# A graph-attention layer on one core: low parts of V summed by one wide product in ten of 32 row tiles

## The chip, the cores and the metric

The kernel runs on one core of a Trainium2 chip. The metric is the device time of one execution in microseconds (us); a time is the median of several runs. A profile is one further execution, recorded by the hardware profiler.

## The reference, cut to what matters

```python
h = jnp.maximum(_layernorm(x, axis=-1), 0.0)          # x is 4096 x 128
h = h @ W.T + b_W
e = (h @ a1)[:, None] + (h @ a2)[None, :] + b_a[0]    # 4096 x 4096
e = jnp.where(e > 0, e, 0.2 * e)
scores = jnp.where(adjacency_matrix > 0, e, -9e15)
attention = jax.nn.softmax(scores, axis=1)
out = x + attention @ h
```

## The kernel before, in words

The 4096 rows of the output are 32 row tiles of 128, in four groups of eight (`GI`, `NG`). For each group the kernel walks over 16 pairs of neighbour tiles (`PAIRS`), so there are 64 pairs in all, numbered `m`. One pair is a piece of the transposed adjacency matrix of 128 x 2048 integers (1 MB), which SP's queue loads. ScalarE (ACT) turns it into a mask (`mask_part`, L379, two halves), VectorE (DVE) makes of mask, a row and a column of exponentials the weights `w` (`weigh`, L459, two halves of 1024), and TensorE (PE) multiplies (`products`, L841 to L847). `w` has four slots (`SLOTS`), so DVE can be up to four pairs ahead of PE; a slot comes free when PE is done with its pair (`mm_done`).

A weight is a 32-bit word that holds two fp16 numbers, a high and a low part, and V (h times the neighbour's factor) is kept in fp16 as a high and a low part too. For each of the 32 neighbour tiles `jt` and each of the eight row tiles `k` of a group PE therefore issues three products with 128 x 128 stationary weights: high weight by high V, high weight by low V, low weight by high V, and all three add up in the same 129 columns of PSUM. The first 128 columns are the sum of rows, the 129th is the sum of the weights, by which the row is divided. V's two parts lie 136 elements apart (`VW`):

```python
nc.tensor.matmul(sums[:, bank, a, :], w16[:, m % SLOTS, col:col + P, 1], V[:, jt, 0, 0:NF], ...)   # L841
nc.tensor.matmul(sums[:, bank, a, :], w16[:, m % SLOTS, col:col + P, 1], V[:, jt, 1, 0:NF], ...)   # L843
nc.tensor.matmul(sums[:, bank, a, :], w16[:, m % SLOTS, col:col + P, 0], V[:, jt, 0, 0:NF], ...)   # L847
```

The order of the work is written out by hand for every engine. In the first 36 us PE also centres x (L805) and makes h (L815), between the first four pairs. DVE prepares exponentials and factors in three parts of the rows (`PARTS`; `scores`, `pack`, `scale_weights`), DVE and ACT make V of the first two chunks (`products` L598, `highs` L369, `lows` L605), GpSimd (POOL) that of the other six (`halves`). In the three later groups DVE inverts the sums of the group before after the first half of pair 5 of a group (`inverse_sums`, L486 to L490); ACT scales its rows out of PSUM after pair 10 (`scale_rows`, L394), POOL adds x (L792), SP stores. The groups alternate between PSUM banks 0 to 2 and 3 to 5; the last has 3 to 7.

The last group ends in pieces: its last three pairs (`ENDS`) are multiplied piece by piece (`PIECES`: 3, 2, 1, 1, 1 row tiles), so that DVE can divide and store one piece (`inverse_last` L504 to L510, `rows` L542) while PE is at the next. Between them DVE tests the sums (`check_sums`, `check_next`, `check_last`), POOL takes the largest of the results, and a flag says whether a slower general form must run, which it doesn't here. The program ends when the stores have landed.

## Time and profile before

| | |
|---|---|
| time, median of 3 runs | 202.33 us (201.9 to 202.39) |
| profiled execution: its own time | 203.52 us |
| profiled execution: span from first to last instruction | 201.9 us |
| PE busy | 197.2 us (98%) |
| DVE busy | 183.1 us (91%) |
| ACT busy | 147.9 us (73%) |
| POOL busy | 53.8 us (27%) |
| moved by DMA | 75.66 MB, mean 375 GB/s |

The profiled execution took 1.62 us more than its span, for what lies around the instructions, and stands 1.19 us above the median of the runs. In the rows, PE is the product itself and PEld the load of its stationary weights; a product is recorded from its start to the modelled end of its result, so that the durations of successive products overlap, and their pace is read from start to start. An fp32 product stands as two records.

### The profile page before, as it was taken

Reading aid. Unit: us, or ns where it says so; the run is one execution under the profiler, and the core shown is the slowest. Engines: PE = TensorE matmul, PEld = TensorE weight load, DVE = VectorE, ACT = ScalarE, POOL = GpSimd, SP = SyncE. Lnnn points to the kernel's source line nnn. Section 1 sums busy time; section 2 is a strip of 40 time slices with the busy share of each in tenths; the row PEclk is TensorE's granted clock in tenths of the full one; section 3 lists DMA queues with packets and bytes.
Section 4 is the critical chain, followed back from the end, with each engine's and each line's share of the span. In section 5 each row is a group of like instructions: output and inputs, shape, how many; then the busy total and the mean of one; then the engine's idle time right before and its main releaser. Section 6 shows DMA issues by size and latency. Waiting matters only on the chain.

```text
span 201.9 us, 7231 instructions
## 1 busy us (share of the span) xinstructions
PE 197.2 (98%) x3183; PEld 190.4 (94%) x3183; DVE 183.1 (91%) x265; ACT 147.9 (73%) x192; POOL 53.8 (27%) x66
## 2 busy tenths in 40 slices
PE   7989999999999999999999999999999999999994
PEld 7558888999999999999999999999999999999994
DVE  4679999999999899987999999989999999999845
ACT  2299988799872777779988688799688888985000
POOL 1000659689997011055000000061000000620000
DMA  5999999999999999999999999999999999996012
GB/s 174 367 412 420 404 411 422 425 406 380 427 428 415 417 424 419 417 425 411 422 419 420 417 417 425 414 420 419 415 419 422 420 414 422 420 356 208 7 38 71
DMA packets 15968, 75.66 MB, mean 375 GB/s; under 512 B 1600, under 2 KB 5952, under 8 KB 7616
## 3 DMA queue, kind: packets, MB, share of 16 engines
q1 hardware_dynamic: 15792, 75.06, 91.3%
q8 instruction: 25, 0.41, 0.8%
q10 hardware_dynamic: 144, 0.13, 0.3%
q14 instruction: 7, 0.06, 0.1%
HBM read 73.08 MB, written 2.11 MB: 372 GB/s over the span
## 4 chain that ended last, share of the span: by engine, by line
PE 97%; ACT 1%; issue 0%; DVE 0%; POOL 0%; POOLq 0%
PE ps L843 29%; PE ps L841 29%; PE ps L847 29%; PE ps L815 4%; PE ps L805 3%; PE ps L857 2%; ACT L411 1%; PE ps L883 1%; ACT hT L335 0%; PE ps L861 0%; PE ps L866 0%; DVE xT L542 0%; PE ps L860 0%; POOL ones L717 0%; ACT warm L411 0%
## 5 line engine op out<-in xcount | busy, mean ns | idle before, releaser
L841 PE MATMUL ps<-V,w 128*128 128x129 f16 x1024 | 174.3, 220 | 0.0
L843 PE MATMUL ps<-V,w 128*128 128x129 f16 x1024 | 174.3, 220 | 0.0
L847 PE MATMUL ps<-V,w 128*128 128x129 f16 x1024 | 174.3, 220 | 0.0
L379 ACT ACTIVATE mask<-adj_sb 128x1024 bf16<-128x1024 int32 x126 | 125.3, 1056 | 27.1 <-DMA adj_sb<-in_adj_t 27.1
L459 DVE SCALAR_TENSOR_TENSOR w<-g_row,pairs,mask 128x1024 f32<-128x1024 f32 x96 | 120.5, 1317 | 5.5 <-ACT mask L379 3.7
L841 PEld LDWEIGHTS ps<-V,w 128*128 128x128 f16 x1024 | 100.2, 98 | 1.5 <-ACT H L340 0.7
L843 PEld LDWEIGHTS ps<-V,w 128*128 128x128 f16 x1024 | 100.2, 98 | 1.0 <-issue 1.0
L847 PEld LDWEIGHTS ps<-V,w 128*128 128x128 f16 x1024 | 100.3, 98 | 0.0
L459 DVE SCALAR_TENSOR_TENSOR w<-ps,pairs,mask 128x1024 f32<-128x1024 f32 x31 | 37.4, 1265 | 0.0
L792 POOL TENSOR_TENSOR xT<-xT,x_sb 128x512 f32<-128x512 f32 x6 | 11.7, 1970 | 76.8 <-ACT xT L394 76.8
L815 PEld LDWEIGHTS ps<-wp,hT 128*128 128x128 f32 x64 | 8.0, 193 | 2.4 <-ACT hT L335 1.7
L805 PE MATMUL ps<-xT,centre 128*128 128x512 f32 x16 | 10.0, 715 | 0.0
L746 POOL TENSOR_TENSOR x_sb<-x_sb,b_row 128x512 f32<-128x512 f32 x8 | 10.0, 1306 | 0.0
L815 PE MATMUL ps<-wp,hT 128*128 128x130 f32 x64 | 8.8, 282 | 0.4 <-ACT hT L335 0.4
L552 DVE BATCH_NORM_STATS2 stats<-x_sb 128x6 f32<-128x128 f32 x32 | 6.8, 280 | 2.5 <-DMA x_sb<-in_x_p 2.5
L761 POOL TENSOR_TENSOR V<-H,evr 128x516 f16<-128x516 f32 (+1 forms) x7 | 6.5, 930 | 5.2 <-DVE evr L591 5.2
L335 ACT ACTIVATE hT<-ps 128x512 f32<-128x512 f32 x8 | 4.7, 588 | 3.7 <-PE ps L805 3.7
L763 POOL TENSOR_TENSOR V<-prod,V 128x516 f16<-128x516 f32 (+1 forms) x7 | 7.0, 1005 | 0.5
L394 ACT ACTIVATE xT<-ps,rg 128x128 f32<-128x128 f32 x24 | 6.5, 381 | 0.0
L762 POOL TENSOR_TENSOR prod<-H,evr 128x516 f32<-128x516 f32 (+1 forms) x7 | 6.5, 925 | 0.0
L795 POOL PARTITION_ALL_REDUCE bad<-bad x1 | 0.4, 380 | 21.7 <-DVE bad L533 21.7
L340 ACT ACTIVATE H<-ps 128x520 f32<-128x520 f32 x8 | 4.7, 593 | 1.6 <-PE ps L815 1.6
(93 smaller groups left out, 62.6 us busy)
## 6 DMA issues: line engine op xcount, KB each, us to landing
adj_sb<-in_adj_t SPq DMA_DIRECT2D x64, 1024.0 KB, 10.5
xT<-in_x_t SPq DMA_DIRECT2D x8, 256.0 KB, 7.2
x_sb<-in_x_p SPq DMA_DIRECT2D x3, 512.0 KB, 10.6
g_row<-g_dram SPq DMA_DIRECT2D x1, 1536.0 KB, 11.0
out<-xT SPq DMA_DIRECT2D x3, 512.0 KB, 9.9
x_sb<-in_x_p SPq DMA_DIRECT2D x2, 256.0 KB, 4.3
out<-xT SPq DMA_DIRECT2D x1, 192.0 KB, 2.0
out<-xT SPq DMA_DIRECT2D x3, 64.0 KB, 1.6
```

The costliest lines, as they stand in the source:

```text
L379: nc.scalar.activation(mask[:, m % MASKS, r], adj_sb[:, m % HELD, r], ACT.Relu, scale=CONNECTED).then_inc(mask_ready, 1)
L394: ins = nc.scalar.activation(Z[:, g, :], sums[:, bank, a, 0:DOUT], ACT.Copy, scale=rg[:, g:g + 1])
L459: nc.vector.scalar_tensor_tensor(w[:, m % SLOTS, side * GC:(side + 1) * GC], g_ps if group == 0 else g_row[:, (group - 1) * GC:group * GC] ...
L552: last = nc.vector.bn_stats(stats[:, g, :], x_sb[:, g, :])
L746: ins = nc.gpsimd.tensor_tensor(x_sb[:, g:g + 4, :], x_sb[:, g:g + 4, :], b_row[:].rearrange("p (a n) -> p a n", a=1).to_broadcast([P, 4, ...
L763: nc.gpsimd.tensor_tensor(V[:, r, 1, 0:NF], prod[:, c % 2, k0:k1, :], V[:, r, 0, 0:NF], ALU.subtract).then_inc(v_ready, 1)
L792: nc.gpsimd.tensor_tensor(Z[:, k, :], Z[:, k, :], x_sb[:, k, :], ALU.add).then_inc(rows_added, 1)
L805: nc.tensor.matmul(ps[:, X_BANK[c], :], centre[:], xT[:, c * CT * P:(c + 1) * CT * P], start=True, stop=True).then_inc(centred, 1)
L815: last = nc.tensor.matmul(ps[:, H_BANK[c] + j // 2, at:at + 2 + DOUT], hT[:, tile * P:(tile + 1) * P], wp[:, WA:WA + 2 + DOUT], start=(j % ...
L841: nc.tensor.matmul(sums[:, bank, a, :], w16[:, m % SLOTS, col:col + P, 1], V[:, jt, 0, 0:NF], start=(jt == 0 and a == 0), stop=False, skip ...
L843: nc.tensor.matmul(sums[:, bank, a, :], w16[:, m % SLOTS, col:col + P, 1], V[:, jt, 1, 0:NF], start=False, stop=False, skip_group_check=True)
L847: last = nc.tensor.matmul(sums[:, bank, a, :], w16[:, m % SLOTS, col:col + P, 0], V[:, jt, 0, 0:NF], start=False, stop=(jt == NT - 1), ski ...
```

## The change

- V's row is laid out anew: 128 low parts, then 128 high parts, then two columns of scale (`NF` is 130 for 128 high parts with the scale), 264 elements in all. The scale is DVE's exponential `ev` itself, as a high and a low fp16 part (`scale_weights`, `ones_low`); before it was a column of H times the same factor as the rest of V. The rest of V is made as before, in 128 columns for 129.
- In ten of the 32 row tiles (`parted`: tile 6 of groups 0 and 2, tiles 0 to 4 of group 1, tiles 0, 2 and 4 of group 3) the products of the high weight with low and high V become one product of 258 columns (`MERGED`), whose low sums stand in 128 PSUM columns of their own. In the other 22 the three products stay, with 130, 128 and 130 columns.
- Groups 1 and 3 now use banks 3 to 7. PE waits for all weights of group 0 before pair 16, since banks 6 and 7 hold a row that `weigh` reads in group 0; and for the scale columns before pairs 0, 4 and 8.
- Of a tile summed apart, ACT scales the low sums too (into `extra`) and POOL adds them; in the last group DVE adds them in `rows`, with a second operation per tile. `inverse_sums` adds the two scale sums with reductions and then inverts; `inverse_last` does so with one operation per tile.
- The pieces of the last group are 2, 2, 2, 1, 1 row tiles.

```diff
-    NF = DOUT + 1
-    VW = DOUT + 8
-
-    S, T, H0, ONE, HC = 0, 1, 2, 2 + DOUT, 3 + DOUT
+    NF = DOUT + 2
+    HI = DOUT
+    VW = HI + NF + 6
+    MERGED = HI + NF
+
+    S, T, H0, HC = 0, 1, 2, 2 + DOUT
...
+    FIRST_OF_PART = tuple(first // 2 for first, _ in PARTS)
...
-    PIECES = ((0, 3), (3, 5), (5, 6), (6, 7), (7, 8))
+    PIECES = ((0, 2), (2, 4), (4, 6), (6, 7), (7, 8))
...
     def sums_at(group, k):
 
 
+        if group % 2 == 0:
+            return (k // 3, k % 3 * NF) if k < 6 else (2, (k - 6) * MERGED)
         if group < NG - 1:
-            return 3 * (group % 2) + k // 3, k % 3
-        return ((3, 0), (3, 1), (3, 2), (4, 0), (4, 1), (5, 0), (6, 0), (7, 0))[k]
+            return (3 + k, 0) if k < 5 else (k - 2, MERGED)
+        return ((3, 0), (3, MERGED), (4, 0), (4, MERGED), (5, 0), (5, MERGED), (6, 0), (7, 0))[k]
+
+    def parted(group, k):
+
+
+        if group % 2 == 0:
+            return k == 6
+        return k < 5 if group < NG - 1 else k in (0, 2, 4)
+
+    apart = [GI * group + k for group in range(NG - 1) for k in range(GI) if parted(group, k)]
...
-        V = sb("V", [P, NT, 2, VW], F16)
+        V = sb("V", [P, NT, VW], F16)
...
+        def high_sums(group, k):
+            bank, at = sums_at(group, k)
+            at += HI if parted(group, k) else 0
+            return ps[:, bank, at:at + NF]
+
+        def low_sums(group, k):
+            bank, at = sums_at(group, k)
+            return ps[:, bank, at:at + DOUT]
+
+        def both_sums(group, k):
+            bank, at = sums_at(group, k)
+            return ps[:, bank, at:at + MERGED]
...
-                        bank, a = sums_at(group, k)
-                        ins = nc.scalar.activation(Z[:, g, :], sums[:, bank, a, 0:DOUT], ACT.Copy, scale=rg[:, g:g + 1])
+                        ins = nc.scalar.activation(Z[:, g, :], high_sums(group, k)[:, 0:DOUT], ACT.Copy, scale=rg[:, g:g + 1])
+                        if parted(group, k):
+                            ins = nc.scalar.activation(extra[:, apart.index(g), :], low_sums(group, k), ACT.Copy,
+                                                       scale=rg[:, g:g + 1])
...
-                    first, bank = GI * group, 3 * (group % 2)
+                    first = GI * group
                     dve.wait_ge(mm_done, PAIRS * (group + 1))
-                    for a, b, k0, k1 in ((bank, 2, 0, 6), (bank + 2, 1, 6, 8)):
-                        of = sums[:, a:a + b, 0:(k1 - k0) // b, DOUT]
+
+                    if group % 2 == 0:
+                        blocks = ((ps[:, 0:2, 0:3 * NF].rearrange("p b (a n) -> p b a n", a=3)[:, :, :, DOUT:NF], 0, 6),
+                                  (ps[:, 2:3, 0:MERGED].rearrange("p b (a n) -> p b a n", a=1)[:, :, :, HI + DOUT:MERGED], 6, 7),
+                                  (ps[:, 2:3, MERGED:MERGED + NF].rearrange("p b (a n) -> p b a n", a=1)[:, :, :, DOUT:NF], 7, 8))
+                    else:
+                        blocks = ((ps[:, 3:8, 0:MERGED].rearrange("p b (a n) -> p b a n", a=1)[:, :, :, HI + DOUT:MERGED], 0, 5),
+                                  (ps[:, 3:6, MERGED:MERGED + NF].rearrange("p b (a n) -> p b a n", a=1)[:, :, :, DOUT:NF], 5, 8))
+                    for of, k0, k1 in blocks:
                         r = slice(first + k0, first + k1)
-                        ins = nc.vector.reciprocal(rden[:, r].rearrange("p (b a) -> p b a", b=b), of)
-                        nc.vector.tensor_copy(den[:, r].rearrange("p (b a) -> p b a", b=b), of)
-                    ins.then_inc(rden_ready, 1)
+                        ins = nc.vector.tensor_reduce(den[:, r].rearrange("p (b a) -> p b a", b=of.shape[1]), of, AX_X, ALU.add)
+                    ins.then_inc(sums_added, 1)
+                    dve.wait_ge(sums_added, group + 1)
+                    nc.vector.reciprocal(rden[:, first:first + GI], den[:, first:first + GI]).then_inc(rden_ready, 1)
...
+                    for k in range(k0, k1):
+                        of = high_sums(NG - 1, k)
+                        ins = nc.vector.tensor_scalar(den[:, first + k:first + k + 1], of[:, DOUT:DOUT + 1],
+                                                      of[:, DOUT + 1:NF], gg[:, 1:2], ALU.add, ALU.mult)
+                    ins.then_inc(sums_added, 1)
+                    dve.wait_ge(sums_added, NG - 1 + i + 1)
+                    nc.vector.reciprocal(rg[:, first + k0:first + k1], den[:, first + k0:first + k1]).then_inc(rg_ready, 1)
...
+                    first = GI * (NG - 1)
+                    split = [k for k in range(*PIECES[i]) if parted(NG - 1, k)]
+                    for k in split:
+                        g = first + k
+                        nc.vector.scalar_tensor_tensor(Z[:, g, :], low_sums(NG - 1, k), rg[:, g:g + 1], x_sb[:, g, :],
+                                                       ALU.mult, ALU.add).then_inc(rows_begun, 1)
                     for k in range(*PIECES[i]):
-                        g = GI * (NG - 1) + k
-                        bank, a = sums_at(NG - 1, k)
-                        ins = nc.vector.scalar_tensor_tensor(Z[:, g, :], sums[:, bank, a, 0:DOUT], rg[:, g:g + 1],
-                                                             x_sb[:, g, :], ALU.mult, ALU.add)
+                        if k not in split:
+                            g = first + k
+                            ins = nc.vector.scalar_tensor_tensor(Z[:, g, :], high_sums(NG - 1, k)[:, 0:DOUT], rg[:, g:g + 1],
+                                                                 x_sb[:, g, :], ALU.mult, ALU.add)
+                    for k in split:
+                        g = first + k
+                        dve.wait_ge(rows_begun, sum(parted(NG - 1, n) for n in range(k + 1)))
+                        ins = nc.vector.scalar_tensor_tensor(Z[:, g, :], high_sums(NG - 1, k)[:, 0:DOUT], rg[:, g:g + 1],
+                                                             Z[:, g, :], ALU.mult, ALU.add)
                     ins.then_inc(rows_ready, 1)
...
-                    nc.vector.reciprocal(H[:, r, ONE], rstd[:, 2, r]).then_inc(ones_ready, 1)
...
+                    nc.vector.tensor_copy(V[:, r, HI + DOUT], ev[:, r]).then_inc(ones_begun, 1)
+
+                def ones_low(part):
+                    r = slice(*PARTS[part])
+                    dve.wait_ge(ones_begun, part + 1)
+                    nc.vector.tensor_tensor(V[:, r, HI + DOUT + 1], ev[:, r], V[:, r, HI + DOUT], ALU.subtract
+                                            ).then_inc(ones_ready, 1)
...
                 products(0)
+                ones_low(0)
...
+                    ins = nc.gpsimd.tensor_tensor(Z[:, k, :], Z[:, k, :], x_sb[:, k, :], ALU.add)
+                    parts = [g for g in apart if k.start <= g < k.stop]
+                    if parts:
+                        step(ins)
+                        e = apart.index(parts[0])
+                        ins = nc.gpsimd.tensor_tensor(Z[:, parts[0]:parts[-1] + 1, :], Z[:, parts[0]:parts[-1] + 1, :],
+                                                      extra[:, e:e + len(parts), :], ALU.add)
+                    ins.then_inc(rows_added, 1)
...
+                    if k0 == 0 and m in FIRST_OF_PART:
+                        pe.wait_ge(ones_ready, FIRST_OF_PART.index(m) + 1)
...
                             col = side * GC + k * P
-                            bank, a = sums_at(group, k)
-                            nc.tensor.matmul(sums[:, bank, a, :], w16[:, m % SLOTS, col:col + P, 1], V[:, jt, 0, 0:NF],
-                                             start=(jt == 0 and a == 0), stop=False, skip_group_check=True)
-                            nc.tensor.matmul(sums[:, bank, a, :], w16[:, m % SLOTS, col:col + P, 1], V[:, jt, 1, 0:NF],
-                                             start=False, stop=False, skip_group_check=True)
-                            last = nc.tensor.matmul(sums[:, bank, a, :], w16[:, m % SLOTS, col:col + P, 0], V[:, jt, 0, 0:NF],
+                            first = jt == 0 and sums_at(group, k)[1] == 0
+                            if parted(group, k):
+                                nc.tensor.matmul(both_sums(group, k), w16[:, m % SLOTS, col:col + P, 1], V[:, jt, 0:MERGED],
+                                                 start=first, stop=(jt == NT - 1), skip_group_check=True)
+                            else:
+                                nc.tensor.matmul(high_sums(group, k), w16[:, m % SLOTS, col:col + P, 1], V[:, jt, HI:HI + NF],
+                                                 start=first, stop=False, skip_group_check=True)
+                                nc.tensor.matmul(low_sums(group, k), w16[:, m % SLOTS, col:col + P, 1],
+                                                 V[:, jt, 0:DOUT], start=False, stop=False, skip_group_check=True)
+                            last = nc.tensor.matmul(high_sums(group, k), w16[:, m % SLOTS, col:col + P, 0], V[:, jt, HI:HI + NF],
                                                     start=False, stop=(jt == NT - 1), skip_group_check=True)
...
+                        pe.wait_ge(w_ready, 2 * PAIRS)
```

On PE, group 0, row tiles 6 and 7 of one neighbour tile (the rows are the products with their output shape; weight loads aren't listed). Before:

```order
L841 MATMUL ps<-V,w 128x129
L843 MATMUL ps<-V,w 128x129
L847 MATMUL ps<-V,w 128x129
L841 MATMUL ps<-V,w 128x129
L843 MATMUL ps<-V,w 128x129
L847 MATMUL ps<-V,w 128x129
```

The change, same place:

```order
L903 MATMUL ps<-V,w 128x258
L910 MATMUL ps<-V,w 128x130
L906 MATMUL ps<-V,w 128x130
L908 MATMUL ps<-V,w 128x128
L910 MATMUL ps<-V,w 128x130
```

Tile 6 has two products for three, 388 columns for 387; tile 7 keeps three, with 388 columns. Over the program PE has 320 products fewer.

On DVE, at the start of the products, from the factors of V (`evr`) to the last of pair 0's weights (`w`). Before:

```order
L591 TENSOR_TENSOR evr<-ev,rstd 128x8 [waits weights_ready]
L598 TENSOR_TENSOR prod<-H,evr 128x516 [waits h_ready,ones_ready,scaled_ready]
L470 SCALAR_TENSOR_TENSOR w<-ps,pairs,mask 128x512 [waits rows_spread,mask_early,pairs_ready]
L605 TENSOR_TENSOR V<-prod,V 128x4x129 [waits high_ready,product_ready]
L470 SCALAR_TENSOR_TENSOR w<-ps,pairs,mask 128x512 [waits rows_spread,mask_early]
L459 SCALAR_TENSOR_TENSOR w<-ps,pairs,mask 128x1024 [waits mask_first]
```

The change:

```order
L636 TENSOR_TENSOR evr<-ev,rstd 128x8 [waits weights_ready]
L638 CAST V<-ev 128x8
L650 TENSOR_TENSOR prod<-H,evr 128x512 [waits h_ready,scaled_ready]
L643 TENSOR_TENSOR V<-ev,V 128x8 [waits ones_begun]
L500 SCALAR_TENSOR_TENSOR w<-ps,pairs,mask 128x512 [waits rows_spread,mask_early,pairs_ready]
L657 TENSOR_TENSOR V<-prod,V 128x4x128 [waits high_ready,product_ready]
L500 SCALAR_TENSOR_TENSOR w<-ps,pairs,mask 128x512 [waits rows_spread,mask_early]
L489 SCALAR_TENSOR_TENSOR w<-ps,pairs,mask 128x1024 [waits mask_first]
```

Two short operations for the scale columns come in, L638 ahead of the product of V and L643 ahead of the first weights.

On DVE, the end of the last group, from the piece that comes before the first test of the sums (before: row tile 5; now: row tiles 4 and 5). Before:

```order
L504 RECIPROCAL rden<-ps 128x1 [waits acc_done]
L506 COPY den<-ps 128x1
L510 TENSOR_SCALAR rg<-rden,gg 128x1 [waits rden_ready]
L542 SCALAR_TENSOR_TENSOR xT<-ps,rg,x_sb 128x128 [waits xb_ready,rg_ready]
L516 TENSOR_SCALAR bad<-den 128x30 [waits gate_ready,den_ready]
L519 TENSOR_REDUCE bad<-bad 128x1 [waits bad_ready]
```

The change:

```order
L542 TENSOR_SCALAR den<-ps,gg 128x1 [waits acc_done]
L542 TENSOR_SCALAR den<-ps,gg 128x1
L546 RECIPROCAL rg<-den 128x2 [waits sums_added]
L579 SCALAR_TENSOR_TENSOR xT<-ps,rg,x_sb 128x128 [waits xb_ready,rg_ready]
L584 SCALAR_TENSOR_TENSOR xT<-ps,rg,x_sb 128x128
L589 SCALAR_TENSOR_TENSOR xT<-ps,rg,xT 128x128 [waits rows_begun]
L554 TENSOR_SCALAR bad<-den 128x30 [waits gate_ready,sums_added]
L557 TENSOR_REDUCE bad<-bad 128x1 [waits bad_ready]
```

The test of the sums now stands behind three row operations instead of one. After it come the pieces of tiles 6 and 7, one row operation each, as before.

## Rows read from the trace of the kernel before

**Rows 1.** The page, part 1: engine, busy us (share of the span), instructions.

```profile
PE 197.2 (98%) x3183; PEld 190.4 (94%) x3183; DVE 183.1 (91%) x265; ACT 147.9 (73%) x192; POOL 53.8 (27%) x66
```

**Rows 2.** The page, part 4: the chain that ended last, share of the span by engine.

```profile
PE 97%; ACT 1%; issue 0%; DVE 0%; POOL 0%; POOLq 0%
```

**Rows 3.** Timeline of PE (start us, us, engine, line): first products of pairs 0, 4; last.

```profile
18.27 0.23 PE L841 MATMUL ps<-V,w 128*128 128x129 f16 x1
...
35.70 0.22 PE L841 MATMUL ps<-V,w 128*128 128x129 f16 x1
...
198.85 0.22 PE L847 MATMUL ps<-V,w 128*128 128x129 f16 x1
```

**Rows 4.** Groups of instructions, 35.6 to 199.2 us: xcount | busy us, mean ns | idle.

```profile
L841 PE MATMUL ps<-V,w 128*128 128x129 f16 x960 | 163.2, 220 | 0.0
```

**Rows 5.** Busy time by stretch, 100 to 110 us: five engines, PEclk, DMA share, GB/s.

```profile
100.00:110.00 10.00, 10.00 (x181) 10.00 (x179) 10.00 (x9) 8.12 (x9) 0.00 (x0) 1.00 1.01 419
```

**Rows 6.** The chain in order of time, start of the program: start us, us, what.

```profile
5.35 0.43 PE ps L861 x2
...
7.69 0.43 PE ps L866 x2
8.12 1.64 PE ps L805 x2
...
16.60 0.90 PE ps L815 x8
17.49 0.86 PE ps L805 x2
```

**Rows 7.** The page, part 5: weight loads, xcount | busy us, mean ns | idle.

```profile
L847 PEld LDWEIGHTS ps<-V,w 128*128 128x128 f16 x1024 | 100.3, 98 | 0.0
L815 PEld LDWEIGHTS ps<-wp,hT 128*128 128x128 f32 x64 | 8.0, 193 | 2.4 <-ACT hT L335 1.7
```

**Rows 8.** Timeline of DVE, start of the products.

```profile
15.50 0.69 DVE L598 TENSOR_TENSOR prod<-H,evr 128x516 f32<-128x516 f32 x1
16.32 0.75 DVE L470 SCALAR_TENSOR_TENSOR w<-ps,pairs,mask 128x512 f32<-128x512 f32 x1
...
18.25 1.27 DVE L459 SCALAR_TENSOR_TENSOR w<-ps,pairs,mask 128x1024 f32<-128x1024 f32 x1
```

**Rows 9.** Timeline of DVE, before pair 7's weights.

```profile
39.22 0.25 DVE L572 RECIPROCAL H<-rstd 128x16 f32<-128x16 f32 x1
39.38 1.19 DVE L459 SCALAR_TENSOR_TENSOR w<-ps,pairs,mask 128x1024 f32<-128x1024 f32 x1
...
41.98 2.46 DVE L459 SCALAR_TENSOR_TENSOR w<-ps,pairs,mask 128x1024 f32<-128x1024 f32 x2
```

**Rows 10.** Timeline of ACT: group 1's rows are scaled.

```profile
131.63 2.16 ACT L394 ACTIVATE xT<-ps,rg 128x128 f32<-128x128 f32 x8
```

**Rows 11.** Timeline of DVE: weights of pairs 43 to 49, [idle before <- releaser].

```profile
134.78 17.92 DVE L459 SCALAR_TENSOR_TENSOR w<-g_row,pairs,mask 128x1024 f32<-128x1024 f32 x14 [0.91 <-ACT mask L379]
```

**Rows 12.** Timeline of DVE, the last three pieces.

```profile
197.52 0.35 DVE L542 SCALAR_TENSOR_TENSOR xT<-ps,rg,x_sb 128x128 f32<-128x128 f32 x1
197.79 0.17 DVE L516 TENSOR_SCALAR bad<-den 128x30 f32<-128x30 f32 x1
197.99 0.19 DVE L519 TENSOR_REDUCE bad<-bad 128x1 f32<-128x32 f32 x1
198.09 0.16 DVE L504 RECIPROCAL rden<-ps 128x1 f32<-128x1 f32 x1
...
199.10 0.17 DVE L504 RECIPROCAL rden<-ps 128x1 f32<-128x1 f32 x1
199.19 0.15 DVE L533 SCALAR_TENSOR_TENSOR bad<-ps,bad 128x1 f32<-128x1 f32 x1
199.31 0.21 DVE L510 TENSOR_SCALAR rg<-rden,gg 128x1 f32<-128x1 f32 x1
199.56 0.35 DVE L542 SCALAR_TENSOR_TENSOR xT<-ps,rg,x_sb 128x128 f32<-128x128 f32 x1
```

**Rows 13.** The page, part 6: the last stores, KB each, us to landing.

```profile
out<-xT SPq DMA_DIRECT2D x3, 64.0 KB, 1.6
```

50 lines of the change are left out of this document (20 added, 30 removed).

## The prediction

> **What bounds the kernel now.** I read the page's first part, the chain that ended last, and then PE's timeline. PE is busy 98% of the span, DVE 91% [rows 1], and the chain is PE's for 97% [rows 2]. A busy PE alone would say little, since overlapping records hide pauses; the pace says more. From pair 4 on there are 60 pairs of 16 row-tile steps (two neighbour tiles, eight row tiles) with three products, 2880 in all, as the groups of instructions confirm with 960 of each kind [rows 4]. The first starts at 35.70 us, the last at 198.85 [rows 3]: 163.15 us over 2879 gaps is 56.67 ns from start to start. At the upper of the two clock levels, 2.4 GHz, which the stretches show as a granted clock of 1.00 [rows 5], that is 136 cycles for 129 columns. An average so near a whole number over four groups leaves no room for waits: from pair 4 on the end is set by the number of products and what one costs, and by a tail of DVE and a store behind the last one. DMA is just as full (share 1.01 at 419 GB/s, [rows 5]), but a pair is 1.05 MB and needs 2.50 us at that rate, while PE takes 48 x 56.67 ns = 2.72 us for it.
>
> **Products.** Of 1024 steps (32 neighbour tiles, 32 row tiles), 320 go from three products with 387 columns to two with 388, and 704 keep three, with 388 columns. 320 products and 320 weight loads disappear. What that is worth hangs on how 136 cycles divide between columns and a fixed part, and on whether it is the product or the load of its weights that paces. No row shows 128, 130 or 258 columns of fp16. The nearest are fp32: records of 512 columns follow at 0.86 / 2 = 0.430 us, of 130 at 0.90 / 8 = 0.1125 us [rows 6]. Over 382 columns the difference is 0.3175 us, 0.83 ns each, so such a record spends two cycles of 2.4 GHz per column; 1024 cycles are 426.7 ns, which leaves about 3.3 ns of fixed part for a record of two passes. I take for one pass of fp16 a fixed part between half of that and the whole, 1.7 to 3.3 ns, the middle being 2.5 ns or 6 cycles. Then 130 cycles are left for 129 columns: the odd column is filled up to an even number. That is the value I use:
> - before, every step 3 x 136 = 408 cycles;
> - three products: 136 + 134 + 136 = 406, so 704 x 2 = 1408 cycles saved;
> - two products: (258 + 6) + 136 = 400, so 320 x 8 = 2560 saved.
>
> 3968 cycles are **1.65 us less**. The bounds: with nothing filled up the fixed part is 7 cycles, steps cost 409 and 402, and 320 x 6 - 704 x 1 = 1216 cycles or 0.51 us are saved; with 1.7 ns (4 cycles) and filling to fours they cost 404 and 400, and 5376 cycles or 2.24 us are saved.
>
> A rule speaks against the change here. The Trainium skill (TensorE: Matmul & The Clock Gate, "Wait — 56ns, not 53.3ns?") gives the gap of products at full clock as columns over 2.4 GHz plus about 2.5 ns, with no filling. For 129 columns that is 56.25 ns, and the row has 56.67 [rows 3]: the fixed part agrees with my middle, the column count does not. By the rule alone a step would go from 168.75 to 169.17 or 166.67 ns, and the sum would be 0.37 us less instead of 1.65.
>
> **Supply.** A quicker PE needs w sooner; I looked where the lead is least. At the start, DVE's product of V begins at 15.50 and lasts 0.69, the first weights begin only at 16.32 [rows 8]: 0.13 us are free, and the new subtraction L643 issues in about 0.1 there (short operations follow one another by 0.09, 199.10 to 199.19 [rows 12]); the copy L638 lies in the wait of the product for `evr`. The second half of pair 0's weights ends at 18.25 + 1.27 = 19.52 [rows 8], and PE wants it 24 gaps after 18.27 [rows 3], at 19.63. I take 0; each tenth by which the cover falls short costs a tenth. Before pair 7, a reciprocal of 0.16 goes (39.22 to 39.38) and two short operations of 0.1 come; its weights begin at 41.98 and the first half ends 1.23 later, at 43.21 [rows 9], while PE gets there 144 gaps after 35.70, at 43.86. Lead 0.65 us; PE will come 0.13 us sooner, so 0.5 stays: cost 0. In group 1, ACT scales eight tiles in 2.16 us, 0.27 each [rows 10]; five more are 1.35 us ahead of the masks, and DVE already waits 0.91 for one of these, of pair 43 [rows 11]. But its weights are ready 1.28 after 134.78, at 136.06, and PE gets to pair 43 at 35.70 + 39 x 2.72 = 141.78. Of 5.7 us lead, 1.35 and some 0.7 of quicker PE go: cost 0. POOL's extra additions lie in its idle time (27% busy, [rows 1]).
>
> **The tail.** Here the change adds. Before, the first sum is read at 199.10 and the last row is written at 199.56 + 0.35 = 199.91 [rows 12], 0.81 us after PE; the last store takes 1.6 us to land [rows 13] and ends the span. Now the last piece costs the same: one TENSOR_SCALAR (0.21, as L510), a reciprocal (0.17), a row (0.35), three waits of 0.03, 0.82 us. But DVE comes late to it. Piece (4, 6) has three row operations, and the test of the sums stands behind them. Counted from PE's end of that piece: two den operations until 0.31, reciprocal 0.34 to 0.51, rows from 0.54, 0.27 apart (197.52 to 197.79), the test at 1.35, its reduction 0.20 later (197.79 to 197.99), the next den 0.10 later, at 1.65. PE has finished tile 6 at 18 x 56.4 ns = 1.02. Its den, reciprocal, row and check take 0.24 + 0.20 + 0.27 + 0.09, so the last den starts at 2.45, when PE was done at 2.03. That is 0.42 us late; with 0.01 for the longer piece I count **0.4 us more**. Bounds: 0, if DVE is quicker and not late, and 0.6, if instead of the store the flag sets the end: its test L569 now stands behind the reciprocal (0.35 after the start of the piece, before 0.09), so it comes 0.42 + 0.26 = 0.7 later, with POOL and the flag behind it.
>
> **Sum.** 203.52 - 1.65 + 0.4 = 202.27 us for the profiled execution, 1.25 less. The median of the runs is 1.19 lower than that execution: 202.33 - 1.25 = **201.1 us**.
>
> **The rivals.** A measurement of this kernel tells 0.3%, 0.61 us, from no change.
> - *The weight load paces.* Early in the program products of 2 columns follow at 0.43 / 2 us, exactly as those of 128 [rows 6]: there the load set the pace, at half the later speed (512 columns took 1.64 / 2, later 0.86 / 2). At full speed that fp32 load would need 0.107 us; fp16 loads are recorded half as long as fp32 ones (98 to 193 ns, [rows 7]), so about 54 ns, just what is needed for 56.67 with some fixed part. Then 128 columns are no quicker than 130, only the 320 lost products count, 8 cycles each, 1.07 us: 202.33 - 1.07 + 0.4 = 201.7. For it: these rows; against it: nothing but that a fixed part of 2.5 ns explains the same pace.
> - *Columns plain.* 0.51 less and 0.4 more: 202.2, no change. For it: 7 cycles are within my bounds for the fixed part; against it: they are nearly all of what two passes of fp32 have (3.3 ns are 8). The Trainium skill's rule above (TensorE: Matmul & The Clock Gate) would come to much the same, 202.33 - 0.37 + 0.4 = 202.4.
> - *Filling to fours.* 202.33 - 2.24 + 0.4 = 200.5. For it only the lower end of the fixed part.
> - *An exposed load: slower.* The weights of the product behind the 258 columns might not be loaded under it. The 41 ns by which a load (98) outlasts a gap (57) would cost 320 x 41 = 13 us, 214 us in all. It decides from 5.9 ns per step on: (1.25 + 0.61) / 320. Against it: fp32 products of 512 columns follow at 0.430 with loads of 193 ns beside them [rows 6, 7], so a long product hides its successor's load.
>
> **How the numbers follow.** My forecast 0.47, load paces 0.28, plain columns 0.09, fours 0.08, exposed load (or another loss of that kind) 0.08. Faster by over 0.3%: nearly all of the first (0.45), all of the fours (0.08), and 0.17 of the second, whose 0.67 us lies just past the bound: 0.70. Slower: 0.08. The rest, 0.22, is no change. Range 200.4 to 202.2: it takes in the fours and the plain columns, and with them both ends of the tail; the slower case and the edges stay out.
>
> **What would show it.** Right: starts of the three products of a common step 169.2 ns in sum, those of a step summed apart 166.7 ns; PE without a pause from pair 0 to the last; the last product 1.6 us earlier; the last den of DVE about 0.4 us after PE is done. If 128 columns still take 56.67 ns, the load paces. Wrong altogether: gaps behind the 258 columns above 110 ns by a load's remainder, or PE waiting for w in groups 0 or 1.

## The result and the profile after

The changed kernel takes 204.94 us (median of 5 runs, 204.52 to 205.27), against 202.33 (201.74 to 203.48) for the kernel before in the same comparison: a ratio of 1.0126, 95% interval 1.0091 to 1.016. It is slower. The forecast was 201.1 us, faster. The profiled execution of after took 204.52 us, with a span of 203.0.

The page of after, parts 1, 3 and 4 (they answer to [rows 1, 2]):

```profile
PE 193.3 (95%) x2863; PEld 183.5 (90%) x2863; DVE 183.7 (91%) x269; ACT 149.3 (74%) x199; POOL 72.2 (36%) x70
...
q8 instruction: 23, 0.38, 0.7%
...
PE 89%; DMA 4%; DVE 2%; SPq 1%; issue 1%; POOL 0%
```

PE is busy 3.9 us less, and the chain is PE's for 89% instead of 97%; POOL is busy 18 us more. The second line, the transfers of an instruction queue (number, MB, share), will be needed below.

After, timeline of PE: the first product, a step summed apart with the step behind it, the last product (answering to [rows 3]):

```profile
16.93 0.23 PE L906 MATMUL ps<-V,w 128*128 128x130 f16 x1
...
179.45 0.27 PE L903 MATMUL ps<-V,w 128*128 128x258 f16 x1
179.56 0.22 PE L910 MATMUL ps<-V,w 128*128 128x130 f16 x1
179.62 0.22 PE L906 MATMUL ps<-V,w 128*128 128x130 f16 x1
179.67 0.22 PE L908 MATMUL ps<-V,w 128*128 128x128 f16 x1
179.73 0.22 PE L910 MATMUL ps<-V,w 128*128 128x130 f16 x1
...
196.22 0.22 PE L910 MATMUL ps<-V,w 128*128 128x130 f16 x1
```

The products start at 16.93 here and at 18.27 in the profile of before; over the profiles of all versions of both kernels that start lies anywhere between 15.86 and 18.82, so I count from the first product. From first to last product: 180.58 us before, 179.29 after, 1.29 less. From the last product's start to the end of the span: 201.91 - 198.85 = 3.06 before, 202.96 - 196.22 = 6.74 after, 3.68 more. Sum 2.39, near the 2.61 between the medians. **The products did get quicker; the end got longer by nearly three times as much.**

What stands at the end is not among the busy groups. After, the instructions at the program's last line by engine (duration in ns, start in us), and ahead of them PE's conditional jump over the slow general form, L1066, of the same trace:

```profile
L1066 PEldq COMPARE_BRANCH  x1: 3346/3346/3346, 199.2 to 199.2; - x1
```

```profile
L291 ACTq DRAIN  x1: 8/8/8, 199.3 to 199.3; - x1
...
L291 SPq DRAIN  x1: 7/7/7, 199.7 to 199.7; - x1
L291 DVEq DRAIN  x1: 61/61/61, 200.0 to 200.0; - x1
L291 PEldq DRAIN  x1: 72/72/72, 202.7 to 202.7; - x1
```

Every other engine is done by 200.1; PE's jump alone takes 3.35 us, and all wait for it. Before, the same jump (L1002):

```profile
L1002 PEldq COMPARE_BRANCH  x1: 471/471/471, 200.9 to 200.9; - x1
```

During the jump of after, the DMA view of 199.3 to 203 us has a transfer of PE's instruction queue; that of before, 200.1 to 202 us, has none:

```profile
q8 instruction: 1, 0.02, 1.6%
```

The page's 23 such transfers carry 0.38 MB, 16 KB each, for some 5,790 instructions of PE (2863 products, 2863 loads, the waits): about 252 instructions each. That this queue is PE's is read from the count. The Trainium skill (Runtime: NRT & Kernel Launch, "Instruction fetch mechanics") says that instructions come in blocks of 256, that prefetch is sequential, and that a taken branch whose target lies outside the two-page window must fetch the target first. Counted in the built programs, the jump stood before at PE's instruction 6425 and went to 6856, from block 25 into 26, the next one. The change takes 640 instructions away ahead of it and adds a wait: 5786 to 6217, from block 22 into 24. (The traces record 6405 and 5766 instructions of PE ahead of the jump, 639 fewer as well.) The distance is the same 431 instructions in both; what differs is the block. The trace agrees with the rule as far as it goes: 0.47 us into the next block, 3.35 with a fetch into the one behind.

The tail of DVE, after (answering to [rows 12]):

```profile
195.68 0.34 DVE L589 SCALAR_TENSOR_TENSOR xT<-ps,rg,xT 128x128 f32<-128x128 f32 x1
195.94 0.17 DVE L554 TENSOR_SCALAR bad<-den 128x30 f32<-128x30 f32 x1
196.15 0.19 DVE L557 TENSOR_REDUCE bad<-bad 128x1 f32<-128x32 f32 x1
196.25 0.28 DVE L542 TENSOR_SCALAR den<-ps,gg 128x1 f32<-128x1 f32 x1
...
197.09 0.28 DVE L542 TENSOR_SCALAR den<-ps,gg 128x1 f32<-128x1 f32 x1
197.40 0.16 DVE L546 RECIPROCAL rg<-den 128x1 f32<-128x1 f32 x1
197.49 0.14 DVE L569 SCALAR_TENSOR_TENSOR bad<-den,bad 128x1 f32<-128x1 f32 x1
197.60 0.35 DVE L584 SCALAR_TENSOR_TENSOR xT<-ps,rg,x_sb 128x128 f32<-128x128 f32 x1
198.19 0.15 DVE L767 TENSOR_SCALAR flag<-bad 128x1 int32<-128x1 f32 x1 [0.23 <-POOL bad L856]
```

The last row is written 197.95 - 196.22 = 1.73 us after the last product's start (before 1.06), and the flag begins 1.97 after it (before 1.04).

POOL, 170 us to the end, after and then before:

```profile
173.90 17.28 POOL L846 TENSOR_TENSOR xT<-xT,x_sb 128x512 f32<-128x512 f32 x2 [33.51 <-ACT xT L421]
191.26 0.46 POOL L851 TENSOR_TENSOR xT<-xT,extra 128x128 f32<-128x128 f32 x1
197.78 0.38 POOL L856 PARTITION_ALL_REDUCE bad<-bad  x1 [6.06 <-DVE bad L569]
```

```profile
173.31 4.51 POOL L792 TENSOR_TENSOR xT<-xT,x_sb 128x512 f32<-128x512 f32 x2 [36.08 <-ACT xT L394]
199.48 0.38 POOL L795 PARTITION_ALL_REDUCE bad<-bad  x1 [21.67 <-DVE bad L533]
```

Two additions of 128 x 512 took 17.28 us instead of 4.51. Of DVE beside them, after and before:

```profile
172.00 16.83 DVE L489 SCALAR_TENSOR_TENSOR w<-g_row,pairs,mask 128x1024 f32<-128x1024 f32 x14
```

```profile
173.18 1.28 DVE L459 SCALAR_TENSOR_TENSOR w<-g_row,pairs,mask 128x1024 f32<-128x1024 f32 x1
174.69 1.98 DVE L459 SCALAR_TENSOR_TENSOR w<-g_row,pairs,mask 128x1024 f32<-128x1024 f32 x1 [0.24 <-PE ps L847]
176.60 2.30 DVE L459 SCALAR_TENSOR_TENSOR w<-g_row,pairs,mask 128x1024 f32<-128x1024 f32 x1
```

Before, the two engines take turns: the first addition ends 1.14 us behind the half that starts at 173.18, the second 1.14 behind the one that starts at 174.69, and the halves that follow take 1.98 and 2.30 us instead of 1.28. After, DVE had lost its lead over PE, waits for no slot of `w` any more and makes 14 halves one behind the other; none of them is stretched, and POOL's first addition, 16.06 us long, ends 1.13 us behind the last of them (188.83). A pause of DVE isn't all that decides who gets a turn: with half loads (below) additions took 2.26 us beside halves without a pause. The Trainium skill (SBUF — State Buffer, "Who interferes with whom") has a rule for this: a DVE instruction with two SBUF inputs contends with a GpSimd instruction that reads SBUF, over a port pair that only one of them can hold. `w` is made there of `g_row` and `mask`, both in SBUF, and the rows above agree; no run took DVE's second input away, so the cause of the 17 us is read from the rows, not tested. What it does to the end was tested, below.

### The profile page after: what moved, and what is told of

The parts are those of the page before. It is cut to its first block, busy times and chain, and to the rows that moved or that the text cites. A ratio compares the mean times of both kernels' runs of the same rounds, so it can differ in the third digit from the quotient of the medians.

```text
span 203.0 us, 6604 instructions
## 1 busy us (share of the span) xinstructions
PE 193.3 (95%) x2863; PEld 183.5 (90%) x2863; DVE 183.7 (91%) x269; ACT 149.3 (74%) x199; POOL 72.2 (36%) x70
## 4 chain that ended last, share of the span: by engine, by line
PE 89%; DMA 4%; DVE 2%; SPq 1%; issue 1%; POOL 0%
PE ps L910 28%; PE ps L906 19%; PE ps L908 19%; PE ps L903 17%; DMA adj_sb<-in_adj_t 4%; PE ps L876 3%; PE ps L866 2%; SPq L297 1%; SPq L302 1%; PE ps L946 1%; DVE den L542 0%; DVE mask L506 0%; DVE rg L546 0%; POOL bad L856 0%; DVE xT L579 0%
## 5 line engine op out<-in xcount | busy, mean ns | idle before, releaser
L910 PE MATMUL ps<-V,w 128*128 128x130 f16 x1024 | 172.7, 220 | 0.0
L906 PE MATMUL ps<-V,w 128*128 128x130 f16 x704 | 129.2, 220 | 0.0
L908 PE MATMUL ps<-V,w 128*128 128x128 f16 x704 | 129.0, 219 | 0.0
L489 DVE SCALAR_TENSOR_TENSOR w<-g_row,pairs,mask 128x1024 f32<-128x1024 f32 x96 | 118.3, 1303 | 5.7 <-ACT mask L407 5.1
L910 PEld LDWEIGHTS ps<-V,w 128*128 128x128 f16 x1024 | 100.2, 98 | 0.0
L903 PE MATMUL ps<-V,w 128*128 128x258 f16 x320 | 73.7, 273 | 0.0
L906 PEld LDWEIGHTS ps<-V,w 128*128 128x128 f16 x704 | 68.9, 98 | 3.9 <-ACT H L369 0.7
L908 PEld LDWEIGHTS ps<-V,w 128*128 128x128 f16 x704 | 68.9, 98 | 1.0 <-issue 1.0
L846 POOL TENSOR_TENSOR xT<-xT,x_sb 128x512 f32<-128x512 f32 x6 | 24.0, 4020 | 74.3 <-ACT xT L421 37.2
L903 PEld LDWEIGHTS ps<-V,w 128*128 128x128 f16 x320 | 31.3, 98 | 1.6
L815 POOL TENSOR_TENSOR V<-H,evr 128x512 f16<-128x512 f32 (+1 forms) x7 | 6.4, 921 | 5.6 <-DVE evr L636 5.6
L866 PE MATMUL ps<-xT,centre 128*128 128x512 f32 x16 | 8.3, 599 | 0.0
L817 POOL TENSOR_TENSOR V<-prod,V 128x512 f16<-128x512 f32 (+1 forms) x7 | 7.2, 1027 | 0.5
L816 POOL TENSOR_TENSOR prod<-H,evr 128x512 f32<-128x512 f32 (+1 forms) x7 | 6.4, 920 | 0.0
```

The costliest lines, as they stand in the source:

```text
L489: nc.vector.scalar_tensor_tensor(w[:, m % SLOTS, side * GC:(side + 1) * GC], g_ps if group == 0 else g_row[:, (group - 1) * GC:group * GC] ...
L817: nc.gpsimd.tensor_tensor(V[:, r, 0:DOUT], prod[:, c % 2, k0:k1, :], V[:, r, HI:HI + DOUT], ALU.subtract).then_inc(v_ready, 1)
L846: ins = nc.gpsimd.tensor_tensor(Z[:, k, :], Z[:, k, :], x_sb[:, k, :], ALU.add)
L866: nc.tensor.matmul(ps[:, X_BANK[c], :], centre[:], xT[:, c * CT * P:(c + 1) * CT * P], start=True, stop=True).then_inc(centred, 1)
L903: nc.tensor.matmul(both_sums(group, k), w16[:, m % SLOTS, col:col + P, 1], V[:, jt, 0:MERGED], start=first, stop=(jt == NT - 1), skip_grou ...
L906: nc.tensor.matmul(high_sums(group, k), w16[:, m % SLOTS, col:col + P, 1], V[:, jt, HI:HI + NF], start=first, stop=False, skip_group_check ...
```

## The experiments

Each is compared with the kernel before in runs on the same chip (medians 201.9 to 202.22 us there); ratios are to that kernel, with 95% intervals. "Tail" is the time from the last product's start to the end of the span in the profile.

**The jump.** First the changed kernel with the code that PE jumps over made shorter, then the kernel before with it made longer; neither touches an instruction that is executed.

```diff
-                    for g in range(NT):
-                        pe.wait_ge(gen_diag, g + 1)
...
+                    with pe.Fori(1, NT) as g:
+                        pe.wait_ge(gen_diag, g + 1)
```

> The changed kernel, with PE's part of the general form (skipped code) shortened from 430 to about 285 instructions by a loop, so that PE's jump at the end lands in the next block of 256 instructions and not in the one after it. Theory A (the jump's target is fetched late; PE's branch took 3.35 us in the changed kernel, 0.47 before): the branch takes about 0.5 us again, the end moves up by 2.6 us to where DVE's drain (200.08) stands, time 202.3 (202.0 to 202.6). Theory B (the later sums, flag and stores of the tail cost the time): no change, 204.9.

```diff
                     pe.wait_ge(gen_t, NT)
+                    for _ in range(64):
+                        nc.tensor.matmul(ps[:, 0, 0:P], ones[:], diag[:], start=True, stop=True)
```

> The kernel before, with 256 instructions more in PE's skipped code, nothing executed is changed. Theory A: the target moves out of the next block, PE's branch takes about 3.3 us instead of 0.47, time 202.3 + 2.7 = 205.0. Theory B: code that is never executed costs nothing, 202.3.

Measured: 201.96 us, ratio 0.9989 (0.9967 to 1.0012), and 205.14 us, ratio 1.0141 (1.0112 to 1.017). The jump in the two traces:

```profile
L1066 PEldq COMPARE_BRANCH  x1: 365/365/365, 199.6 to 199.6; - x1
```

```profile
L1002 PEldq COMPARE_BRANCH  x1: 3982/3982/3982, 199.5 to 199.5; - x1
```

The slowdown goes with the jump in both directions: shortened, the changed kernel is even with before; lengthened, the kernel before loses 1.4%. With the short jump the tail is 4.10 us instead of 6.74. What stayed open is why the repaired kernel gains nothing, with products that pace as forecast.

**The parts of the change.** No tile summed apart (aligned layout, products of 130, 128 and 130 columns, pieces of before), and tiles apart only in the first three groups (seven, pieces of before, short jump):

```diff
...
-        return k < 5 if group < NG - 1 else k in (0, 2, 4)
+        return False
...
```

> The changed kernel with V's new layout and 130, 128, 130 columns in all 32 row tiles: no tile summed apart, pieces 3, 2, 1, 1, 1 as before, PE's instruction count and jump as before. Expected from the pace (128 columns 55.8 ns for 56.7): 1024 x 2 cycles = 0.85 us less in the products; the tail 0.1 to 0.5 us more, as the last test of the sums stands behind a reciprocal. Theory A: branch 0.5 us, time 201.6 to 202.1. Theory B, in which it is the work of merging (ACT, POOL, DVE) that costs: the same, 201.6 to 202.1; what tells here is the tail without the second row operations.

```diff
...
-        return k < 5 if group < NG - 1 else k in (0, 2, 4)
+        return k < 5 and group < NG - 1
...
```

> The changed kernel with the short jump, and with the merged products only in the seven tiles of groups 0 to 2; the last group has three products per step and the pieces 3, 2, 1, 1, 1 of before. Products: 704 - 0 steps... in numbers 0.85 us for the layout and 7 x 32 x 6 cycles = 0.56 us for the merging, 1.41 us less, of which up to 0.36 may be given back in waits before pair 8; tail 0.1 to 0.5 us more. Theory A: 201.0 to 201.8. Theory B (merging in groups 0 to 2 costs through ACT and POOL): 202.3 or more.

Measured: 202.28 us, 1.0013 (0.999 to 1.0036), and 201.69, 0.9975 (0.9959 to 0.999). The layout alone quickens the products (180.05 us from first to last) and loses as much in the tail (3.58). Seven tiles apart, with the last group left as it was, are the first version that is faster than the kernel before, by 0.25%.

**What PE waits for.** With the short jump, PE's gap before pair 3 (in which it makes a chunk of h) was 2.53 us instead of 1.86, and there was one of 0.61 at pair 27. The rows of pair 27, ACT, DVE and PE:

```profile
91.49 1.89 ACT L421 ACTIVATE xT<-ps,rg 128x128 f32<-128x128 f32 x7
93.23 0.40 ACT L423 ACTIVATE extra<-ps,rg 128x128 f32<-128x128 f32 x1
...
94.88 5.52 DVE L489 SCALAR_TENSOR_TENSOR w<-g_row,pairs,mask 128x1024 f32<-128x1024 f32 x4 [1.73 <-ACT mask L407]
...
96.66 0.29 PE L903 MATMUL ps<-V,w 128*128 128x258 f16 x1 [0.39 <-DVE w L489]
```

ACT scales rows, the masks come late, DVE waits, PE waits. The gap before pair 3 in the same run, ACT and then PE:

```profile
25.65 2.01 ACT L407 ACTIVATE mask<-adj_sb 128x1024 bf16<-128x1024 int32 x2 [1.75 <-DMA adj_sb<-in_adj_t]
...
28.05 0.59 ACT L364 ACTIVATE hT<-ps 128x512 f32<-128x512 f32 x1
```

```profile
28.69 1.16 PE L876 MATMUL ps<-wp,hT 128*128 128x130 f32 x8 [0.45 <-ACT hT L364]
```

PE waits for `hT`, which ACT makes behind the mask of pair 3, and that mask waits for its adjacency load. Three edits of the short-jump version: scale columns ahead of `evr` in the second and third part; rows scaled four pairs later (`SCALE_AT` 10 to 14); 20 of the adjacency loads halved. The last two also on the kernel before.

> The changed kernel with the short jump, and in parts 1 and 2 DVE writes the two scale columns ahead of the factors that start POOL's products of V, not behind them. Theory C (the subtraction for the low scale column takes 1.04 us instead of 0.19 because it falls under POOL's first product, and holds up the weights of pair 3): it takes about 0.2 us, PE's gap before pair 3's h falls from 2.53 (short jump alone) to 1.86 us; the time falls by what is not given back at pair 27, 0 to 0.6 us, 201.4 to 202.0. Rival D (masks come late from the loads): the gap before pair 3 stays.

> The changed kernel with the short jump, and ACT scales the rows of the group before after pair 14 of a group instead of after pair 10, where the lead of the masks is larger. Theory D (what PE gained is given back at pair 27, because ACT's scaling comes when the loads of the adjacency matrix leave no lead): PE's wait of 0.6 us before pair 27 goes, products shorter by 0.5 to 1.0 us, time 201.2 to 201.6. Rival (the wait is due to the early start of this run, and later ones take its place): the wait moves to pair 31, time as with the short jump alone, 202.0.

> The kernel before, with the rows scaled after pair 14. PE never waits there, so theory D expects no change, 202.0; if the scaling itself cost time, it would be faster.

> The changed kernel with the short jump; of 20 of the 64 adjacency pieces (pairs 8 to 19 and 24 to 31) only the first half is loaded, the other half of the slot keeps what an earlier pair left there. Theory D (what PE gained is given back in waits for masks whose loads come no earlier): the wait before pair 27 goes, that before pair 3 stays (its load is a whole one), products 179.3 to 179.7 us instead of 180.2; time 201.4 (201.2 to 201.7). Rival (the waits have another cause): 202.0.

> The kernel before with the same half loads of 20 pieces. Theory D: no wait of PE to remove, products 180.58 us as ever, time unchanged at 202.0 to 202.2. If loads had set the time before too: faster.

Measured, in that order: 201.98 us, 0.9994 (0.9973 to 1.0014); 202.08, 1.0003 (0.9984 to 1.0023); 202.12, 0.9992 (0.9975 to 1.0009); 201.76, 0.9977 (0.9961 to 0.9993); 202.19, 1.0011 (0.9983 to 1.004). With the rows scaled later there is no wait at pair 27 and the products take 179.54 us; the time stays. That the edit removed the wait isn't shown: the profile of the change itself, whose products start as late (16.93, here 16.90; with the short jump alone 16.15), has none either, and in the run with seven tiles below whose products start at 15.86 PE waits 0.17 us at pair 31 instead. The subtraction of the scale column falls from 1.05 to 0.20 us when it comes ahead of POOL's product, but the gap before pair 3 stays (2.39): it was not its cause. Over all 20 profiles the gap follows the rows above: `hT` starts 2.38 to 2.40 us behind the mask of pair 3, and the gap is 1.86 or 1.87 wherever it starts up to 11.28 us after the first product, 2.09 at 11.47 and 3.00 at 12.37. So it is the landing of pair 3's load, counted from the start of the products, that varies; the half loads begin at pair 8 and don't touch it (2.15). They bring the changed kernel 0.2% below the kernel before, but not clear of the short jump alone, and nothing in the kernel before. None of these edits brings the time down beyond the noise against the short jump.

**The tail.** The tests between the pieces made ahead of them (those of tiles 24 to 30 left out), then seven tiles apart with scale columns first, rows scaled later and the last test ahead of the last reciprocal; then the same with the fourth adjacency load moved ahead of two others:

> The changed kernel with the short jump; the tests of the sums that stand between the last pieces are made before the first piece, on groups 0 to 2 alone. The test of row tiles 24 to 30 is left out. Theory E (DVE comes late to the last piece because three row operations and the tests don't fit into the 1.02 us that PE needs for one tile): the last den starts 0.3 us after PE's end instead of 0.6, the end moves up by 0.3 to 0.4 us, 201.6. Rival (the flag and POOL's reduction set the end, and they depend on the last sum alone): under 0.15 us.

> Seven tiles apart, none in the last group, with the short jump, the scale columns first, the rows scaled after pair 14, and the last test of the sums ahead of the last reciprocal. If the three losses named (late jump, waits at pairs 3 and 27, tail) are all there is: products 1.41 us shorter than before without waits, tail 0.2 us longer, 202.0 - 1.2 = 200.8 (200.5 to 201.2). If the loads of the adjacency matrix set the time as soon as PE is quicker: 201.5 or more.

> Seven tiles apart, none in the last group, short jump, scale columns first, rows scaled after pair 14, last test ahead of the last reciprocal, and the load of the adjacency piece of pair 3 ahead of the last loads of x. Theory D: the gap before pair 3 is 1.86 us as in the kernel before, no wait at pair 27, products 179.2 us in every run, also in those that start early; tail 0.4 to 0.8 us longer than before. Time 201.0 (200.7 to 201.5). Rival (something later in the chain binds next): 201.7 or more.

Measured: 201.91, 0.9988 (0.9967 to 1.001); 202.1, 0.9991 (0.9971 to 1.0011); 202.29, 0.9997 (0.9976 to 1.0017). The first writes its last row 1.35 us after the last product's start instead of 1.73, the third 1.31, and the end does not follow. DVE and POOL at the end of the third:

```profile
196.29 0.16 DVE L569 SCALAR_TENSOR_TENSOR bad<-den,bad 128x1 f32<-128x1 f32 x1
...
198.66 0.15 DVE L768 TENSOR_SCALAR flag<-bad 128x1 int32<-128x1 f32 x1 [1.75 <-POOL bad L857]
```

```profile
198.25 0.38 POOL L857 PARTITION_ALL_REDUCE bad<-bad  x1 [6.12 <-issue]
```

The test is done at 196.45, the reduction over the partitions begins 1.80 us later, 6.12 us behind POOL's last addition. In between stand only two records of POOL's sequencer, of the reduction's line:

```profile
L857 POOLq MODIFY_POOL_CONFIG  x2: 14/14/14, 192.3 to 192.3; - x2
```

In seven profiles with late additions it began 6.06 to 6.8 us behind the last of them and 5.8 to 6.6 us behind these records; where POOL was free early, the records stood right behind the last addition too, and it began 0.14 us behind the test. So the reduction seems to be prepared in that time; what is done in it no run shows. Whether gains made on PE or DVE end in this wait is tested next.

**The flag without POOL.** PE sums the test results of the 128 rows in one product of one column, and DVE makes the flag from the sum:

```diff
-                pool.wait_ge(bad_ready, 4)
-                nc.gpsimd.partition_all_reduce(bad[:, NT + 4:NT + 5], bad[:, NT + 2:NT + 3], P, RMAX).then_inc(bad_ready, 1)
+                pe.wait_ge(scaled_rows, 2 * (NG - 1))
+                pe.wait_ge(bad_ready, 4)
+                nc.tensor.matmul(ps[:, 0, 0:1], ones[:], bad[:, NT + 2:NT + 3], start=True, stop=True).then_inc(bad_ready, 1)
...
-                nc.vector.tensor_scalar(flag[:], bad[:, NT + 4:NT + 5], 1.0, None, ALU.add).then_inc(flag_ready, 1)
+                nc.vector.tensor_scalar(flag[:], ps[:, 0, 0:1], 0.5 - P, None, ALU.is_gt).then_inc(flag_ready, 1)
```

> The changed kernel with the short jump; POOL's last reduction over the partitions is gone, instead PE sums the 128 rows' test results in one fp32 product of one column, and DVE makes the flag from that sum. Theory (POOL's reduction, which starts 6.1 us and more after POOL's late last addition, holds the flag): in the short-jump run it began 0.27 us after its input, and 0.14 where POOL was free early; the way over PE should start at once and be no longer than the reduction's 0.38, so the flag comes 0.2 to 0.4 us earlier and the time falls from 202.0 to about 201.7, not more, since SP's last store ends 0.3 us before the end there. Rival (the flag is not what ends the program): 202.0, no change. A pause of 6 us between POOL's last addition and whatever POOL does next would show as POOL's late read of the flag.

> The version with seven tiles apart, scale columns first, later row scaling, the last test ahead of the reciprocal and the fourth adjacency load early, with the same flag over PE. In its run with the reduction the last test ended at 196.45 and the reduction began at 198.25, 1.80 us later, 6.12 after POOL's last addition. Theory: with the flag over PE it is made by about 196.9 instead of 198.8; then the last store (issued 196.9, landed 198.5) ends the program at about 198.9 of span instead of 200.6, and the time falls from 202.3 to about 200.6, faster than both kernels. Rival (POOL's pause of 6 us follows its last addition whatever comes next, and the end still waits for POOL): POOL reads the flag only at 198.3 and the gain is 1.1 us or less. Rival (something else holds the end): 202.3.

> Control: the kernel before with the flag over PE. Its POOL was free 21 us ahead, and its reduction began 0.14 us after its input; the last store ends its span. Theory and rival: no change beyond 0.3% against the kernel before, 202.1. If it gains 0.6 us or more, the way over PE is worth something by itself and the gains of the other three must be counted without it.

> Seven tiles apart, scale columns first, later row scaling, the last test ahead of the reciprocal, loads in the old order, flag over PE. In its run with the reduction this began 0.49 us after its input. Theory: the flag comes 0.4 to 0.7 us earlier, SP's last store sets the end, 0.4 us less: about 201.7 against 202.1. If the fourth adjacency load's place is worth nothing this is as fast as the version with it (200.6).

Measured, in that order: 201.77 us, 0.9998 (0.9974 to 1.0021); 200.88, 0.996 (0.9929 to 0.9992); 202.1, 1.0007 (0.9988 to 1.0027); 201.08, 0.9949 (0.9931 to 0.9967). The end of the second, DVE and then PE:

```profile
196.49 0.16 DVE L569 SCALAR_TENSOR_TENSOR bad<-den,bad 128x1 f32<-128x1 f32 x1
...
197.19 0.16 DVE L768 TENSOR_SCALAR flag<-ps 128x1 int32<-128x1 f32 x1
```

```profile
195.80 0.22 PE L908 MATMUL ps<-V,w 128*128 128x130 f16 x1
196.80 0.35 PE L985 MATMUL ps<-bad,ones 128*128 128x1 f32 x2 [0.78 <-DVE bad L569]
```

From the end of the test to the flag it is 0.54 us, as long as over a POOL that is free (before: 199.34 to 199.89), so the control on the kernel before shows nothing; where POOL is late it takes out the wait. POOL reads the flag at 197.38, as soon as it is made and 5.76 us behind its last addition, sooner than any reduction began: the pause doesn't follow an addition whatever comes next. The tail of this run is 3.37 us, and that without the early load 3.36, against 5.04 and 3.72 with the reduction. Without the early load the medians fall by 1.0 us and the two intervals don't overlap; the profiles show 0.36 of it; the one with the reduction is of a run 0.7 us above its median, and the rest was seen in no profile. The early load is worth nothing that these runs can tell. Both versions are faster than the kernel before, by 0.4 and 0.5%. With ten tiles apart and the short jump alone the gain stays away: the flag begins 0.14 us earlier, not 0.2 to 0.4 (1.94 instead of 2.08 us after the last product's start), and the test itself ends 1.40 us after that start, against 0.85 with seven. With the test ahead of the reciprocal, as in the versions with seven, it still ends 1.34 after it (ten with every repair, below): two row operations per tile apart stand in DVE's last pieces.

**How many tiles.** All repairs, with ten and with no tiles apart:

> All ten tiles apart with every repair of the version that took 201.08 (short jump, scale columns first, row scaling later, last test ahead of the reciprocal, flag over PE). Theory: against seven tiles apart 96 more steps save 8 - 2 = 6 cycles each, 0.24 us, but the three tiles apart of the last group put two row operations of 0.3 us each into the last pieces, and DVE was 0.4 us later with its last row there (1.73 us after the last product's start against 1.3): 201.1 to 201.3. Rival (the tail's extra row operations cost nothing once the flag is not on POOL): 200.8.

> The same repairs with no tile apart: the aligned layout alone, three products of 130, 128 and 130 columns in every step, pieces of before. Theory (each product paces by its own columns, and with the waits and the flag repaired the time follows the products): 1024 x 2 cycles less than before, 0.85 us, against 1.41 with seven tiles apart, so 0.5 to 0.6 us above that version: about 201.6, 0.4 to 0.5 us below before. Rival (the tiles apart save nothing once the repairs are made, and the repairs are the whole gain): 201.1, as with seven.

Measured: 201.27 us, 0.9966 (0.9939 to 0.9993), and 201.56, 0.9983 (0.9962 to 1.0005), with seven 201.08 as above. The medians stand in the order that the theory has, but the intervals of ten and seven overlap; that seven are better than ten is not shown. Without tiles apart the interval reaches past 1, and it touches that of seven: that summing apart adds to the repaired layout is borne out by the products (179.32 against 179.86 us, 0.54 less where the theory has 0.56) rather than by the times. Tails: 3.85 us with ten, 3.36 with seven, 3.37 with none; the products with ten take 179.58. In these stands one pause of 0.5, in which PE waits for the last weights: their two halves took 2.30 and 2.29 us beside POOL's addition.

## Why the prediction was wrong

- **The pace: right.** Starts behind 130 columns follow at 56.67 ns on average, behind 128 at 55.8, behind 258 at 110, in all 320 cases: 169.2 and 166.7 ns per step, the forecast's values. 129 columns took what 130 take, so the odd column was filled up, and at 2.4 GHz each of the three leaves 2.5 ns, the 6 cycles of fixed part. Neither the load nor plain columns set the pace, filling to fours didn't occur, and no load was exposed behind 258 columns. The rule of the Trainium skill that the prediction set beside it (TensorE: Matmul & The Clock Gate) gives 56.67 for 130 columns, 55.83 for 128 and 110 for 258, all as measured; it fails for the odd 129 of before alone (56.25, measured 56.67).
- **Supply: cost 0 was too low.** Of 1.65 us, 0.36 were lost: 0.23 before pair 3, 0.11 before pair 7, 0.02 before pair 1. At pair 7, in group 0, the text had 0.5 us of lead left, and PE waited for `w`, one of its signs of being wrong. The short operations there cost DVE no more than the text has; DVE came to them 0.5 us later (its operation `st` ahead of pair 6's second half starts 38.46 - 34.54 = 3.92 us after pair 4's first product, before 39.11 - 35.70 = 3.41). Before pair 3 the text had not looked; there PE waits for h behind the mask of pair 3, whose load landed late, as above. The subtraction L643 was put at 0.1 us; it took 0.19, and 1.05 in the second part, beside a POOL operation.
- **The tail: right mechanism, too small.** The text had +0.4 us with bounds of 0 and 0.6; without the jump it is 4.10 - 3.06 = 1.04. The term that was too small is the den operation at 0.21 (as L510): it reads two columns of PSUM and takes 0.28, and the next one follows it by 0.20. The two of piece (4, 6) take 0.48 instead of 0.31, and the last den started 0.87 after the last product's start instead of 0.67 as its "0.42 us late" has it. And the flag, named as an upper bound, does set the end with the short jump: in that profile DVE's drain, behind the flag, ends at 200.24, SP's, behind the last store, at 199.87. The flag begins 1.04 us later than before, where the text has 0.7: 0.20 of the difference is the den, 0.13 the reduction, which began 0.27 behind the test instead of 0.14.
- **POOL: wrong.** "POOL's extra additions lie in its idle time" took POOL's idle share for free time. One of its additions got no turn beside 13 halves of `w`, the last ended 14 us later than before, and the reduction behind them came late. In the profile of the change itself that cost nothing yet (the reduction began at 197.78, 0.15 behind the test, as where POOL is free), but it swallowed the repairs: the same version takes 202.1 us with the reduction and 201.08 without (ratios 0.9991 and 0.9949), with the early load 202.29 and 200.88 (0.9997 and 0.996).
- **The end of PE's program: the step that failed.** No term and no rival had it; the sum takes the last store as the end and puts PE's own way there at nothing. The text counted 320 products and 320 loads as time removed, and not as instructions ahead of a jump. Measured, the jump takes 3.35 us instead of 0.47, and these 2.9 us outweigh every gain: shortening the skipped code alone took the changed kernel from 204.94 to 201.96 us. The sum by what was measured, in the profiles: 183.64 us from first product to end before, -1.29, +1.04, +2.64 for the jump, 186.03.

The slower rival had the right sign for a reason that did not occur. Two slips in the text change nothing: (1.25 + 0.61) / 320 is 5.8 ns, not 5.9, and the upper bound of the tail, 0.6, lies below the 0.7 that it works out for the flag.

## What to carry to other kernels

A change that adds or removes many instructions moves every later jump against the blocks in which code is fetched: look at the duration of the branch at the end of each engine, and keep what it jumps over short. An engine that is idle is not free if its work has to take turns with another's; before giving it more, see how long its operations take while the other is busy. When a quicker stage brings nothing, follow the last instruction back in the new profile: here the gain was held by a jump, by a longer tail on DVE and by a late reduction on POOL. With the jump shortened and the last group left alone 0.25% showed, with the other repairs and the reduction gone 0.5%.

## What was not expected of the hardware

- A taken jump of PE cost 0.37 to 0.49 us into the next block of instructions and 3.35 to 3.98 us into the one behind it.
- An addition of 128 x 512 fp32 on POOL took 1.29 us on average where `b_row` is added, 2.3 where it took turns with DVE's halves of `w` (which then took up to about 2.3 instead of 1.28), and 16 where it got no turn; and a subtraction of 128 x 8 on DVE 1.05 instead of 0.19 beside POOL.
- POOL's reduction over the partitions did not begin sooner than 6.06 us behind POOL's last operation, though its input was ready; a product on PE did the same without that pause.
